# A decoder layer on one core: a new order of steps in its attention stage, and the maximum subtracted in the exponential alone

## The reference

```
q, k, v = x @ Wq + bq, x @ Wk + bk, x @ Wv + bv
scores  = (q k^T + c2p + p2c) / sqrt(24)     # c2p, p2c: q and k against 64 position keys, gathered by distance
out     = softmax(scores) v @ Wo + bo + x
out     = layernorm(out) * scale + bias      # the sublayer's own norm
x       = layernorm(x + out)                 # then the outer one
```

## Time and profile before

| | |
|---|---|
| runs | 2840.59, 2842.94, 2843.41 us (median 2842.94) |
| the profiled execution's own time | 2838.59 us |
| its span, first to last instruction | 2836.9 us |
| busy: PE, ACT, DVE, POOL | 2414.7, 2286.8, 2232.0, 711.7 us |
| POOL L352 (take_max) | 128 of 1042 ns |
| ACT L593 (one exponential) | 128 of 634 ns |
| ACT L596 (a quarter of a unit) | 512 of 391 ns |
| DVE L749 (second_norm) | 56 in the loop, mean 532 ns |
| first DVE instruction | 26.14 us from the start |
| attention stage ends, experts stage runs | 950 us; about 1400 to 2780 us |

### The profile page before, as it was taken

How to read it: one execution, slowest core, us unless ns; L and a number is a source line. 1 busy time by engine, 2 the same in 40 slices (tenths; PEclk the granted TensorE clock), 3 DMA queues, 4 the chain that set the end, 5 groups by cost and what they waited for, 6 DMA issues and landing times. The chain is left out here.

```text
span 2836.9 us, 64292 instructions
## 1 busy us (share of the span) xinstructions
PE 2414.7 (85%) x18180; PEld 1323.1 (47%) x18199; DVE 2232.0 (79%) x6591; ACT 2286.8 (81%) x4255; POOL 711.7 (25%) x565
## 2 busy tenths in 40 slices
PE   2888888888888337746699999999999999999997
PEld 1555555555555226614344444444444444444443
DVE  3788888788888576785488888888888888888887
ACT  1888888888888353317699999999999999999997
POOL 2334534544444101124311111111111111111114
PEclk7899999999999659977799999999999999999999
DMA  2000000000000100000011111211111121111113
GB/s 78 13 22 12 11 17 16 11 13 20 11 11 12 44 0 1 0 30 0 16 45 53 52 45 45 60 45 45 52 52 45 45 60 45 45 53 51 45 45 89
DMA packets 182540, 96.04 MB, mean 34 GB/s; under 512 B 22539, under 2 KB 179291, under 8 KB 182491
## 3 DMA queue, kind: packets, MB, share of 16 engines
q1 hardware_dynamic: 182491, 95.45, 12.0%
HBM read 78.10 MB, written 4.73 MB: 29 GB/s over the span
## 5 line engine op out<-in xcount | busy, mean ns | idle before, releaser
L1955 DVE TENSOR_TENSOR c_Hl<-c_HF,c_Hh 128x512 f16<-128x512 f32 x1028 | 679.6, 688 | 160.9 <-ACT c_Hh L1842 144.7
L1838 ACT ACTIVATE c_HF<-c_H,c_b 128x512 f32<-128x512 f32 x1028 | 711.0, 692 | 64.2 <-PE c_H L1777 44.3
L1842 ACT ACTIVATE c_Hh<-c_H,c_b 128x512 f16<-128x512 f32 x1028 | 706.4, 687 | 0.0
L1893 POOL TENSOR_TENSOR c_EX<-c_euler,c_D 128x16 f32<-128x16 f32 x65 | 188.6, 2902 | 1194.6 <-DVE c_D L1928 1194.6
L1775 PE MATMUL c_H<-c_Ch,SH 128*128 128x512 f16 x1028 | 390.1, 379 | 0.0
L1777 PE MATMUL c_H<-c_Ch,SH 128*128 128x512 f16 x1028 | 390.0, 379 | 0.0
L1776 PE MATMUL c_H<-c_Cl,SH 128*128 128x512 f16 x1028 | 390.0, 379 | 0.0
L1786 PE MATMUL c_Y<-c_Hh,SH 128*128 128x512 f16 x1024 | 388.1, 379 | 0.3 <-DVE c_Hl L1955 0.3
L1788 PE MATMUL c_Y<-c_Hl,SH 128*128 128x512 f16 x1024 | 388.1, 379 | 0.0
L1787 PE MATMUL c_Y<-c_Hh,SH 128*128 128x512 f16 x1024 | 388.1, 379 | 0.0
L692 DVE CUSTOM_DVE_ANT_0 a_T<-a_S,a_POS 128x128 f32<-128x128 f32 x1024 | 234.8, 285 | 48.0 <-PE a_S L436 41.0
(11 more groups left out here) (300 smaller groups left out, 4372.8 us busy)
## 6 DMA issues: line engine op xcount, KB each, us to landing
c_CWB<-c_rows SPq DMA_DIRECT2D x260, 256.0 KB, 4.1
a_QN<-a_QH SPq DMA_DIRECT2D x128, 32.0 KB, 1.9
a_KN<-a_KH SPq DMA_DIRECT2D x128, 32.0 KB, 1.8
out<-d_O SPq DMA_DIRECT2D x16, 256.0 KB, 2.3
a_QN<-a_QL SPq DMA_DIRECT2D x64, 32.0 KB, 1.9
a_KN<-a_KL SPq DMA_DIRECT2D x64, 32.0 KB, 1.8
CUR<-in_ctx SPq DMA_DIRECT2D x1, 1848.0 KB
c_rows<-c_CWR SPq DMA_DIRECT2D x65, 8.0 KB, 1.4
```

The source lines that it names most:

```text
L1838: act.activation(HF[:, k % 4, :], bH[k % 4][:, :], ACT.Gelu_apprx_tanh, bias=b1[:, g % EXPERTS, f:f + 1], scale=1.0 / WSCALE).then_inc(hf_ ...
L1842: act.activation(Hh[:, g % 2, f, :], bH[k % 4][:, :], ACT.Gelu_apprx_tanh, bias=b1[:, g % EXPERTS, f:f + 1], scale=1.0 / WSCALE).then_inc( ...
L1955: dve.tensor_tensor(Hl[:, g % 2, f, :], HF[:, k % 4, :], Hh[:, g % 2, f, :], ALU.subtract)\
```

## The change

- `EARLY_MAX` becomes empty: POOL's subtraction goes, and all 16 units take four exponentials with the bias.
- Tiles: one at step 5, one at step 6, two at each of steps 7 to 13 (`TILE_STEPS`). The semaphores of QN and KN are split by group of heads, so a tile waits for three DMAs and not for twelve.
- k is projected at step 2 instead of 1. ACT's high halves come after the exponentials of units 1 and 2, DVE's low halves at steps 2 and 3. v is projected one sequence a step at steps 10 to 13, and `values_in` is at step 14 instead of 2.
- `second_norm` is at step 14 instead of 9. POOL's `power` calls keep their order. `residuals` waits for the last block's `first_norm` only, so on POOL it comes right after the second `power`, and `spread_keys` has nothing ahead of it but its own waits.
- Start: the four first sequences of x are loaded on their own, the next four behind them, and Wo, the biases and the rest of x last, under semaphores of their own. The engines begin when the first ten loads are in. POOL copies the first block of x before the five large memsets.

```diff
-NORM_STEPS = (2, 3, 4, 5, 6, 7, 9)
+NORM_STEPS = (2, 3, 4, 5, 6, 7, 14)
+TILE_STEPS = (5, 6, 7, 7, 8, 8, 9, 9, 10, 10, 11, 11, 12, 12, 13, 13)
+V_STEPS = (10, 11, 12, 13)
-CONSTS, TAB, BUILT = 21, 10, 4
+CONSTS, FILLS, TAB, BUILT = 16, 5, 10, 4
-EARLY_MAX = range(6, 14)
+EARLY_MAX = range(0, 0)
...
+def tiles_of(u):
+    return [n for n, step in enumerate(TILE_STEPS) if step == u]
...
-        qn_in, kn_in = Count(sem("qn_in"), 16 * 3 * NG), Count(sem("kn_in"), 16 * 3 * NG)
+        qn_in, kn_in = ([Count(sem(n + str(g)), 16 * 3) for g in range(NG)] for n in ("qn_in", "kn_in"))
...
-                for src, dst in loads + late:
+                for src, dst in loads:
                     sp.dma_start(dst, src).then_inc(loaded, 16)
+                for n in range(2):
+                    sp.dma_start(X[:, n * NB:(n + 1) * NB, :], tokens[:, n * NB:(n + 1) * NB, :]).then_inc(x_in, 16)
+                    if n == 0:
+                        sp.wait_ge(x_in, 16)
+                for src, dst in late:
+                    sp.dma_start(dst, src).then_inc(late_in, 16)
...
# POOL
-            def residuals(i):
-                hold(pool, spare_pool, link_s.sem, link_s.at(i, 0))
+            def residuals(i, first):
+                if not first:
+                    hold(pool, spare_pool, link_s.sem, link_s.at(i, -3))
...
-            pool.wait_ge(loaded, LOADS)
+            pool.wait_ge(x_in, 16)
             copy_block(0, 0)
+            pool.wait_ge(xb.sem, 1)
+            pool.memset(table[96:128, :, :, :, :], 0.0).then_inc(filled, 1)
...
             def body(i, first=False, last=False):
                 if not last:
                     copy_block(i, 1)
-                if not first:
-                    power(i - 1, 0)
                 for u in range(UNITS):
                     if u in EARLY_MAX:
                         take_max(i, u)
-                    if u == NORM_STEPS[5] and not first:
-                        power(i - 1, 1)
-                residuals(i)
+                    if u in (NORM_STEPS[1], NORM_STEPS[5]) and not first:
+                        power(i - 1, (NORM_STEPS[1], NORM_STEPS[5]).index(u))
+                residuals(i, first)
                 if not last:
                     spread_keys(i, 1)
                     values_out(i, 1)
...
# PE
                     if u == 1 and not last:
-                        project_qk(i, 1)
+                        project_q(i, 1)
                     if u == 2 and not last:
-                        project_v(i, 1)
+                        project_k()
+                    if u in V_STEPS and not last:
+                        project_v(V_STEPS.index(u))
...
# ACT
+                    if u in (1, 2) and not last:
+                        high_half(i, 1, u - 1)
...
# DVE
-                    if u == 1 and not last:
-                        low_half(i, 1, 0)
-                        low_half(i, 1, 1)
-                    if u == 2 and not last:
+                    if u in (2, 3) and not last:
+                        low_half(i, 1, u - 2)
+                    if u == 14 and not last:
                         values_in(i, 1)
                     if u in NORM_STEPS and not first:
                         norm_step(i - 1, NORM_STEPS.index(u))
```

More of the change, by code:

```diff
@@ L293, in spread_keys @@
                     hold(pool, spare_pool, s_ps.sem, s_ps.at(i, UNITS))
-                hold(pool, spare_pool, qn_in.sem, qn_in.at(i, qn_in.per * (1 + nxt)))
-                hold(pool, spare_pool, kn_in.sem, kn_in.at(i, kn_in.per * (1 + nxt)))
+                for done in qn_in + kn_in:
+                    hold(pool, spare_pool, done.sem, done.at(i, done.per * (1 + nxt)))
                 pool.tensor_copy(QS[:, :, :, :], QN[:, :, :, :].rearrange("p g s b -> p g b s"))
@@ L356, in body @@
             def body(i, first=False, last=False):
+                if first:
+                    pool.wait_ge(x_in, 32)
+                    pool.wait_ge(late_in, LATE)
                 if not last:
                     copy_block(i, 1)
-                if not first:
-                    power(i - 1, 0)
                 for u in range(UNITS):
@@ L386, in transposes, with project_q, project_k, project_v @@
                 last.then_inc(xT_ps.sem, 1)
-            def project_qk(i, nxt):
+            def project_q(i, nxt):
                 pe.wait_ge(xT_ok.sem, xT_ok.at(i, 1 + nxt))
                 pe.matmul(bG[0][:, :], Wq[:, :], xT[:, ::-1, :], start=True, stop=True).then_inc(qk_ps.sem, 1)
+            def project_k():
                 pe.matmul(bG[1][:, :], Wk[:, :], xT[:, :, :], start=True, stop=True).then_inc(qk_ps.sem, 1)
[L393 to L396, removed]
+            def project_v(b):
+                pe.matmul(bM[:, b * S:(b + 1) * S], xT[:, :, b], Wv[:, :], start=True, stop=True).then_inc(v_ps.sem, 1)
             def bucket_tile(i, nxt, n):
@@ L485, in _ @@
             pe.wait_ge(consts, CONSTS)
-            pe.wait_ge(loaded, LOADS)
+            pe.wait_ge(loaded, EARLY)
             pe.sem_inc(et_ps.sem, et_ps.credit)
@@ L500, in _ @@
             pe.wait_ge(tab, 5)
-            project_qk(0, 0)
-            project_v(0, 0)
+            project_q(0, 0)
+            project_k()
+            for b in range(NB):
+                project_v(b)
             pe.wait_ge(tab, TAB)
@@ L527, in body @@
                     if u == 1 and not last:
-                        project_qk(i, 1)
+                        project_q(i, 1)
                     if u == 2 and not last:
-                        project_v(i, 1)
-                    for n in range(2 * (u - 6), 2 * (u - 6) + 2):
-                        if 0 <= n < TILES and not last:
+                        project_k()
+                    if u in V_STEPS and not last:
+                        project_v(V_STEPS.index(u))
+                    for n in tiles_of(u):
+                        if not last:
                             bucket_tile(i, 1, n)
@@ L562, in high_half @@
                 if nxt:
-                    done = (qn_in, kn_in)[n]
-                    act.wait_ge(done.sem, done.at(i, done.per))
+                    for done in (qn_in, kn_in)[n]:
+                        act.wait_ge(done.sem, done.at(i, done.per))
                 act.activation((QH, KH)[n][:, :], bG[n][:, :], ACT.Identity, bias=(bq, bk)[n][:, :])\
@@ L610, in _ @@
             act.wait_ge(consts, CONSTS)
-            act.wait_ge(loaded, LOADS)
+            act.wait_ge(loaded, EARLY)
             act.sem_inc(e_ok.sem, e_ok.credit)
@@ L626, in body @@
                         x_columns(i, 1)
-                    if u == 1 and not last:
-                        high_half(i, 1, 0)
-                        high_half(i, 1, 1)
                     if 0 <= u - 3 < UNITS:
                         exp_columns(i, u - 3)
-                    for n in range(2 * (u - 6), 2 * (u - 6) + 2):
-                        if 0 <= n < TILES and not last:
+                    for n in tiles_of(u):
+                        if not last:
                             high_rows(i, 1, n)
@@ L656, in low_half @@
                 if nxt:
-                    done = (qn_in, kn_in)[n]
-                    dve.wait_ge(done.sem, done.at(i, done.per))
+                    for done in (qn_in, kn_in)[n]:
+                        dve.wait_ge(done.sem, done.at(i, done.per))
                 dve.scalar_tensor_tensor((QL, KL)[n][:, :], bG[n][:, :], (bq, bk)[n][:, :], (QH, KH)[n][:, :],
@@ L779, in _ @@
             dve.wait_ge(consts, CONSTS)
-            dve.wait_ge(loaded, LOADS)
+            dve.wait_ge(loaded, EARLY)
             for a in range(3):
@@ L868, in body @@
                         norm_step(i - 1, NORM_STEPS.index(u))
-                    for k in range(2 * (u - 6), 2 * (u - 6) + 2):
-                        if 0 <= k < TILES and not last:
+                    for k in tiles_of(u):
+                        if not last:
                             split_rows(i, 1, k)
```

47 lines of the change are left out of this document (29 added, 18 removed).

## The result

The changed kernel takes **2893.01 us** (median of 4 runs, 2890.21 to 2894.94) against 2842.01 (2840.59 to 2843.41). The ratio is 1.0179, with a 95% interval of 1.0161 to 1.0196: slower by 1.8%. The forecast was 2900. The profiled execution took 2894.50, its span 2892.8, with a mean granted clock of 0.927 (0.939 before).

The account below looks back on a forecast made before the run. Bound by waits between hand-written orders. 2838.6 - 19.5 (start) - 1.3 (first and last block) + 78 (fourteen blocks at 5.6) = 2895.8, plus 4 from profiled execution to median: 2900 us; range 2822 to 2918.

Parts of the forecast that it names:

- What bounds the kernel: One block of the stage changed: no engine is full; the waits between the engines' hand-written orders bound it.
- ACT, steps 0 to 13: ACT gets 5.1 us more work, sets the pace from step 7 at 2.8 a step; unit 14 starts 1.8 us earlier.
- rival (d): ACT as new bound: steps 0 to 7 stall by 3.3, +35 us on top of another case; chance 0.05.
- The interleaving: Steps 14 and 15: one POOL KD instruction gets in between each pair of second_norm's four; first chunk 5.9 us later.
- (a): second_norm's four instructions pass together once QS ends: +0.2 us a block, 2825 us in all; chance 0.20.
- (b): Only one or two KD get in among second_norm's four: +2.3 or +4.4 us a block, 2855 to 2884; chance 0.17.
- When QS starts: Step 14: POOL's QS starts at about 447.8, 0.7 us before DVE issues second_norm.
- The price with four waits: second_norm waits for QS and three KD, at most 7.9 us in all; first chunk 5.9 us later in a block.
- Behind the chunk: The tail is the same work; 0.3 us a block less because PE and ACT have nothing old left.
- The start: Earlier first instruction -15.8, memsets beside DVE's copies +2, earlier first tile -5.7: -19.5 us in all.
- First and last block: Block 0, without a norm, +1 us; the last, without tiles and spread_keys, -2.3; together -1.3.
- POOL's saving: POOL's own saved work counts nothing, as POOL waits anyway.

Follow-up runs that it names:

- The run in which QS leads: Changed kernel with POOL's eight waits on the stacking DMAs moved in front of its wait for the scores of unit 15: 2939.9 us, ratio 1.0351.
- The run with the filler: Changed kernel with four extra 128x512 products on PE at the head of step 16, their result unused: 2870.91 us, ratio 1.0109.

## Why the prediction came out, point by point

- **What bounds the kernel: right.** The runs moved by waits between hand-written orders. Adding 4 us a block to ACT's work did nothing to the time in the old order (1.0004, with the clock's help), nor did taking the added work off again in the new one, with the norm at 9.
- **ACT, steps 0 to 13: the pace right, the gain too large.** From step 7 on ACT sets the pace: it takes 2.8 a step, without a wait, as worked out (starts of L627 at 451.76 and 454.54). Unit 14 comes 35.95 after the copy of x on average (35.64 in the block shown); forecast 35.4. But the 37.2 of before was no usual block: three of the fourteen have it, those with a whole stretch at the low clock inside their steps, and the mean is 36.64. The gain is 0.7 a block and not 1.8. That ACT's new work would not become a loss, rival (d), was right (the norm at 9: 2809).
- **The interleaving: right, and shown.** Between each two instructions of `second_norm` one of POOL's gets in, at 7.93 us in all when QS leads, as worked out. As mechanisms, rivals (a) and (b) fall: where POOL's instructions stand ready, they use every gap. By its count the changed kernel is rival (b)'s case, one KD between two of DVE's, but because QS came late and not because gaps were passed over.
- **When QS starts: wrong.** The prediction put QS 0.7 before `second_norm`, and so four waits. It missed the eight waits that `spread_keys` puts between the scores and QS, 0.84 us in all when nothing covers them, of the 1.1 by which it was off. QS came 0.42 after the first of the four, two slipped through, and two waited: 4.66 us instead of 7.9. The chunk came 3.84 later, and not 5.9.
- **The price with four waits: too low.** The run in which QS leads is the forecast's own case, and it took 2939.9, above the stated range. There the chunk comes 7.1 later than before (46.86 against 39.72) and not 5.9. The forecast had counted from a block whose chunk stood at 40.28, it had unit 14 too early, and it let `add_positions(15)` follow `second_norm` at once, where it comes 0.41 later in all these runs.
- **Behind the chunk: wrong sign.** I took 0.3 off because nothing old is left to do. It was +1.34, since in PE's 4.15 us without work the granted clock falls to 0.50 and stays there for 6.8 us. The run with the filler shows it: 1.6 us a block returned. These errors nearly cancel, +5.14 a block against +5.6. That 2900 came so close to 2893 is luck: the mechanism was right, but two waits too many made up for a price too low and a tail of the wrong sign.
- **The start: right.** The second copy of x came 19.0 earlier; forecast 19.5. The memsets cost about 2.2 (L823 1.37; L833 and L834 1.22 and 1.16), forecast 2.
- **First and last block.** Block 0 +1.6, forecast +1. The last was not measured by itself; taking the block before it like the others, about -1.3 is left for it, forecast -2.3. The 4 us carried over from the profiled execution to the median had no counterpart: the changed kernel's median is 1.5 below its profiled execution.
- **POOL's saving: not quite nothing.** In the old order, and with the norm at 9, giving up the subtraction leaves the time where it is. With the norm at 14 it is worth 21 us, as POOL then stands in front of fewer of DVE's instructions.

The 51 us, from runs: the start gave 17.7 and the place of `second_norm` cost 84, some 22 of that through the clock. What is left, about 16 faster, must be the rest of the change (when tiles, k and v are made, and the exponentials); its parts were not run by themselves. The best versions are the change with the norm at step 9, with or without the subtraction: 2809 and 2807, 1.1% under the kernel before.

## What to carry to other kernels

Before a short run of VectorE passes is moved, look at what GpSimd does at that place: passes of 0.34 us became 2.1 us each, because a long GpSimd instruction came in between each two, and everything queued behind them was late. The remedy can be one step in the order, a wait on GpSimd, or a form of the instruction that doesn't share. And an idle TensorE can be paid twice, once in the wait and once in the clock that follows. Last, take the 'before' of a sum from several blocks: one block, picked here, stood 0.6 us a block off the mean.

## What the runs showed of the hardware that was not expected

- Which engine gets in depends on more than who issued first. Between L779, 0.26 us apart, POOL got in each time (4.66, 6.81, 7.93 us by how many of its instructions stood ready). DVE's row of 512 columns in the earlier trace rows, 0.34 apart, held POOL out instead. The prediction's reason, that the ports are free for longer between the short ones, was only argued; no run changed the spacing or the size.
- Waits that are already met cost POOL 0.84 us for eight, with what each `hold` does beside the wait, when the engine is idle, and nothing where an instruction of POOL was running (the norm at 14 with the subtraction).
- Filling TensorE's pause with matmuls that nobody reads made the kernel 22 us faster.
- Two kernels of equal time, before and with the subtraction given up in the old order, differ in how long TensorE sits at its low clock: 3.4 and 0.8 us a block. A low stretch behind the chunk makes that part 15.2 us long instead of 14.1.
